# Narrower level products and transposes in a four-layer graph network on one core

## The reference, cut to what matters

```python
x = _layernorm(x + L0(x, edge_index, ...))               # GCN after a two-layer MLP
x = _layernorm(x + L1(x, edge_index, edge_weight, ...))  # two weighted GCN convolutions
x = _layernorm(x + L2(x, src, dst, ...))                 # attention over the edges of a node
x = _layernorm(x + L3(x, src, dst, edge_attr, ...))      # edge MLP, segment sum, update MLP
# inside L0
h = relu(nodes @ W1 + b1) @ W2                           # 64 -> 128 -> 64
msgs = h[src] * norm[:, None]
out = segment_sum(msgs, dst, n) + b2
```

## Time and profile before

| | |
|---|---|
| median of 3 runs | 3193.22 us (3192.8 to 3195.03) |
| span of the profiled execution | 3193.3 us (the profile gives no other time for it) |
| PE busy | 2310.1 us, 72% |
| DVE busy | 2033.0 us, 64% |
| ACT busy | 1390.8 us, 44% |
| POOL busy | 2135.9 us, 67% |
| mean granted clock of PE | 0.864 |

### The profile page before, as it was taken

The page is one execution under the profiler, slowest core; times in us unless marked ns, Lnnn a source line. Parts: engine busy times, 40 slices in busy tenths (PEclk is TensorE's granted clock), DMA queues, the critical chain, the costliest instruction groups (busy, mean ns, idle before and its releaser), DMA issues.

```text
span 3193.3 us, 41332 instructions
## 1 busy us (share of the span) xinstructions
PE 2310.1 (72%) x11332; PEld 1296.4 (41%) x11332; DVE 2033.0 (64%) x4224; ACT 1390.8 (44%) x2605; POOL 2135.9 (67%) x1658
## 2 busy tenths in 40 slices
PE   0678999987767986566567885999666476666665
PEld 0233444433325875454434443444344333333332
DVE  4357888877757865555549995777779733333332
ACT  2576777755433332222224544777533233223232
POOL 6457787788810185888868885888432378888887
PEclk9899999988888998788879997999877577777777
DMA  7894222356544543344434453444256622222221
GB/s 227 252 294 112 54 54 55 70 119 135 120 91 100 120 89 74 81 95 101 97 70 116 114 118 72 104 103 102 70 141 158 154 64 59 54 54 54 54 59 25
DMA packets 598244, 325.99 MB, mean 102 GB/s; under 512 B 510673, under 2 KB 559303, under 8 KB 598020
## 3 DMA queue, kind: packets, MB, share of 16 engines
q1 hardware_dynamic: 524419, 276.68, 33.7%
q0 software_dynamic: 73600, 46.68, 8.8%
HBM read 187.96 MB, written 134.18 MB: 101 GB/s over the span
## 4 chain that ended last, share of the span: by engine, by line
POOL 44%; PE 18%; issue 16%; DMA 8%; DVE 8%; SPq 4%; ACT 2%; DVEq 0%; ACTq 0%; POOLq 0%
POOL g_row L717 34%; POOL out_rows L724 6%; PE bank L831 4%; PE bank L909 4%; DMA x_with_info<-wide 4%; POOL l_a L717 4%; PE pair L889 3%; DVE rT L1526 2%; SPq L600 1%; DMA l_b<-t_x 1%; PE bank L900 1%; PE bank L933 1%; DMA g_row<-t_x,gidx 1%; DVE ss L1452 1%; DVE x_r L1513 1%
## 5 line engine op out<-in xcount | busy, mean ns | idle before, releaser
L717 POOL DMA_INDIRECT g_row<-t_x,gidx x600 | 795.4, 1326 | 237.6 <-issue 201.8
L1142 ACT ACTIVATE hid<-pair,b_up 128x1000 f32<-128x1000 f32 x350 | 378.7, 1082 | 53.6 <-PE pair L890 51.1
L909 PE MATMUL bank<-hid,w_dn 128*64 128x500 f32 x700 | 389.3, 639 | 2.0 <-ACT hid L1142 2.0
L910 PE MATMUL bank<-hid,w_dn 128*64 128x500 f32 x700 | 389.3, 639 | 0.0
L889 PE MATMUL pair<-xT,w_top 64*128 64x500 f32 x500 | 304.1, 691 | 13.9 <-ACT hid L1142 7.3
L717 POOL DMA_INDIRECT g_row<-t_h,gidx x200 | 257.1, 1285 | 79.6 <-issue 60.7
L890 PE MATMUL pair<-xT,w_bot 64*128 64x500 f32 x500 | 304.4, 692 | 0.0
L717 POOL DMA_INDIRECT g_row<-x_with_info,src_i x200 | 259.7, 1299 | 62.3 <-issue 56.7
L724 POOL DMA_INDIRECT out_rows<-n_r,fidx x200 | 248.5, 1242 | 64.8 <-issue 60.3
L724 POOL DMA_INDIRECT x_with_info<-info_r,sidx x200 | 243.1, 1215 | 60.9 <-issue 60.9
L717 POOL DMA_INDIRECT l_a<-in_x,dst_i x88 | 116.5, 1324 | 243.2 <-PE bank L831 216.7
(11 more groups left out here) (264 smaller groups left out, 5618.5 us busy)
## 6 DMA issues: line engine op xcount, KB each, us to landing
x_in<-in_x_cols SPq DMA_DIRECT2D x100, 250.0 KB
x_with_info<-wide SPq DMA_DIRECT2D x50, 476.0 KB
wide<-in_x SPq DMA_DIRECT2D x50, 448.0 KB
out_rows<-x_r SPq DMA_DIRECT2D x100, 224.0 KB
l_k<-keep_row SPq DMA_DIRECT2D x150, 125.0 KB
t_x<-x_r SPq DMA_DIRECT2D x75, 224.0 KB
t_x<-n_r SPq DMA_DIRECT2D x150, 112.0 KB
l_a<-t_x SPq DMA_DIRECT2D x150, 112.0 KB
```

What stands on the lines that cost most here:

```text
L717: return g.indirect_dma_start(out=to, out_offset=None, in_=table, in_offset=bass.IndirectOffsetOnAxis(ap=index[:, tile:tile + 1], axis=0), ...
L909: T.matmul(run.down[0:D, 0:CH], w_dn[a.stage][:, 0:D], hid[a.b2][:, 0, :], start=True, stop=True)
L910: T.matmul(run.down[D:128, 0:CH], w_dn[a.stage][:, 0:D], hid[a.b2][:, 1, :], start=True, stop=True)\
L1142: A.activation(hid[a.b2][:, :, :], run.up[a.b2][:, :, 0:CH], ACT.Relu, bias=b_up[:, a.stage:a.stage + 1]).then_inc(Cn["hid"], 1)
```

## The change

In levels A, B, C and G and in one product of M, matrices and tiles are cut to the columns and rows in use: 64, or 65 where a row of ones carries a bias or a sum. Nothing else is changed; the buffers, their zeros, the waits and the order stay.

```diff
-            def tiles_to_cols(dst, src):
+            def tiles_to_cols(dst, src, width=128):
                 for k in range(TC):
-                    mm = turn(dst[:, k * R:(k + 1) * R], src[:, k * 128:(k + 1) * 128], R, 128)
+                    mm = turn(dst[0:width, k * R:(k + 1) * R], src[:, k * 128:k * 128 + width], R, width)
...
             def cols_to_tiles(dst, src):
                 for k in range(TC):
-                    mm = turn(dst[0:R, k * 128:(k + 1) * 128], src[:, k * R:(k + 1) * R], 128, R)
+                    mm = turn(dst[0:R, k * 128:k * 128 + D], src[0:D, k * R:(k + 1) * R], D, R)
...
-            def down_rows(dst, h, w):
+            def down_rows(dst, h, w, depth=128, width=D):
                 for k in range(TC):
-                    mm = T.matmul(dst[0:R, 128 * k:128 * k + 128], h[:, k * R:(k + 1) * R], w[:, :], start=True, stop=True)
+                    mm = T.matmul(dst[0:R, 128 * k:128 * k + width], h[0:depth, k * R:(k + 1) * R], w[0:depth, 0:width],
+                                  start=True, stop=True)
...
-                    tiles_to_cols(XT, l_a[q]).then_inc(LA["xdT"].sem, 1)
+                    tiles_to_cols(XT, l_a[q], D).then_inc(LA["xdT"].sem, 1)
...
-                    T.matmul(HT[:, 0:CH], w_top[0][:, :], lxT[q][:, :], start=True, stop=True).then_inc(LA["up"].sem, 1)
+                    T.matmul(HT[:, 0:CH], w_top[0][0:D, :], lxT[q][0:D, :], start=True, stop=True).then_inc(LA["up"].sem, 1)
...
-                        mm = T.matmul(AT[0:R, i * 128:(i + 1) * 128], agg[p][:, i * R:(i + 1) * R], cmat[:, :],
+                        mm = T.matmul(AT[0:R, i * 128:i * 128 + D], agg[p][0:D, i * R:(i + 1) * R], cmat[0:D, 0:D],
                                       start=True, stop=True)
...
-                    down_rows(XC, lxT[q], x_up).then_inc(LA["xc"].sem, 1)
+                    down_rows(XC, lxT[q], x_up, D + 1).then_inc(LA["xc"].sem, 1)
...
-                    down_rows(AT, agg[p], g_out).then_inc(LE["aggT"].sem, 1)
+                    down_rows(AT, agg[p], g_out, D + 1, D + 1).then_inc(LE["aggT"].sem, 1)
...
-                        to, tile = OT[0:R, 128 * i:128 * i + 128], slice(i * R, (i + 1) * R)
-                        T.matmul(to, lhid2[p][:, tile], w_dn[2][:, :], start=True, stop=False)
-                        mm = T.matmul(to, l_in[q][:, tile], x_dn[:, :], start=False, stop=True)
+                        to, tile = OT[0:R, 128 * i:128 * i + D], slice(i * R, (i + 1) * R)
+                        T.matmul(to, lhid2[p][:, tile], w_dn[2][:, 0:D], start=True, stop=False)
+                        mm = T.matmul(to, l_in[q][:, tile], x_dn[:, 0:D], start=False, stop=True)
```

More of the change, by code:

```diff
@@ L953, in slot_a @@
                     at_least(pe, LA["agg"], k)
-                    tiles_to_cols(MT, m_r[p]).then_inc(LA["msgT"].sem, 1)
+                    tiles_to_cols(MT, m_r[p], D).then_inc(LA["msgT"].sem, 1)
                     at_least(pe, LA["xcol"], k + 1)
                     at_least(pe, LA["hid"], k)
-                    T.matmul(HT[:, 0:CH], w_top[0][:, :], lxT[q][:, :], start=True, stop=True).then_inc(LA["up"].sem, 1)
+                    T.matmul(HT[:, 0:CH], w_top[0][0:D, :], lxT[q][0:D, :], start=True, stop=True).then_inc(LA["up"].sem, 1)
                 if c := at(2):
@@ L982, in slot_b @@
                     at_least(pe, LB["ucol"], k)
-                    tiles_to_cols(UT, u_r[p]).then_inc(LB["uT"].sem, 1)
+                    tiles_to_cols(UT, u_r[p], D).then_inc(LB["uT"].sem, 1)
                 if c := at(1):
@@ L987, in slot_b @@
                     at_least(pe, LB["agg"], k)
-                    tiles_to_cols(MT, m_r[p]).then_inc(LB["msgT"].sem, 1)
+                    tiles_to_cols(MT, m_r[p], D).then_inc(LB["msgT"].sem, 1)
                 if c := at(2):
@@ L1002, in slot_b @@
                     at_least(pe, LB["hid"], k)
-                    T.matmul(HT[:, 0:CH], w_top[1][:, :], lxT[p][:, :], start=True, stop=True).then_inc(LB["up"].sem, 1)
+                    T.matmul(HT[:, 0:CH], w_top[1][0:D, :], lxT[p][0:D, :], start=True, stop=True).then_inc(LB["up"].sem, 1)
             lagged_slots(slot_b, 5)
@@ L1011, in slot_c @@
                     at_least(pe, LC["agg"], k)
-                    tiles_to_cols(MT, m_r[p]).then_inc(LC["msgT"].sem, 1)
+                    tiles_to_cols(MT, m_r[p], D).then_inc(LC["msgT"].sem, 1)
             def after_c(at):
```

## The result

The change made the kernel slower: 3386.93 us median (3381.19 to 3392.59, 4 runs) against 3194.12 us before on the same chip, a ratio of 1.0594 with a 95% interval of 1.0569 to 1.0620. The profiled execution spans 3390.8 us, 197.5 more than before; its mean granted clock is 0.763 instead of 0.864. Lines of `kernel.py` behind L933 are one higher than before (the up product L957 is now L958, L964 is L965).

What follows compares the result with a forecast made beforehand. PE was taken to bound only A's first half, gathers B, C and M, with DVE busy most of G. The sum was 3193.3 + 184 (A) + 12 (B) + 12 (C, G, M) = 3401 us, range 3206 to 3460.

Steps and rivals of the forecast that it cites:

- The clock in A: Level A: granted clock stays at 0.50, chunks of 8.9 us on PE, +184 us (+150 to +210).
- the likeliest case: Level A: low clock throughout, 3401 us for the whole kernel; chance 0.66.
- The rival with a risen clock: Level A: clock rises as before, 3217 us (3200 to 3245); chance 0.20.
- Its reason: Start of A: no group fills the array any more, so nothing that came before the clock's rise is left.
- The narrow passes: A's 24 passes a chunk streaming 64 columns: paced by weight loads, gaining only 0.10 us a chunk.
- The rival of passes at half their time: A's narrow passes: loads don't bind, 0.055 us a pass, 3177 us; chance 0.05.
- The changes of shape: Level A: three a chunk at 0.145 us, 0.44 at the high clock (0.25 to 0.60); 0.5 at the low.
- the 0.04 us that do go from the fifth group: A's chunk: the fifth group's excess over the fourth, a wait that a later PE hides, 0.04 us less.
- the rival of two passes: A's turned tiles: turning into 64 columns costs two passes, 10.6 us a chunk, 3490 us; chance 0.04.
- B: Level B: at the low clock PE slightly exceeds the gathers, 6.7 us a chunk against 6.5; +12 us (0 to +25).
- C, G and M: These levels: less PE work may lower their clock, mostly covered by other engines; +12 us together (0 to +60).

Runs made afterwards that it cites:

- the kernels with 64 and 65 rows: Kernel before with only A's up product cut from 128 rows of weights to 64 (ratio 1.0025) or to 65 (ratio 1.0005).
- the last burst: Changed kernel plus unread full products in A, back to back: twelve at chunks 4 and 20 (3350.39 us), or eight at each of seven chunks (3297.57 us).

## Why the prediction came out as it did

**The clock in A**, the likeliest case, is what happened: 0.50 throughout, 8.75 us a chunk against 8.9, PE-bound over all 50 chunks, +177 us against +184. The rival with a risen clock gave 3217 us, 24 more than before; the kernel with its up product whole shows what it would have looked like, 20 more (3222.29 us against 3202.26 of before on its chip).

**Its reason was partly wrong.** I wrote that the tiles use half of the columns, the up product half of the rows, and the narrow passes stream half of the time, and that nothing of what preceded the rise is left. The tiles' columns had no part in it: cut alone they change nothing, and made whole in the changed kernel they bring nothing back. Rows and streams together bring the clock down; A's up product alone is enough to bring it up again. Since columns were cut in turned tiles only, it stays open whether columns don't matter or turned tiles matter less than other products. That the clock "never does in A" is true of this kernel, but closer than I thought: once other products had raised it, the same work held it for 56 us.

The Trainium skill ("TensorE: Matmul & The Clock Gate", "What's actually happening") has the clock follow how busy the array has been. Read as the busy time of the profile, the traces disagree: 94.30 of 94.30 us busy, at 0.50 after the change and at 1.00 before.

**The narrow passes** take what they took before, as the earlier trace rows said: 0.21 us at the low clock, 0.109 at the high one. That the load of 125 columns sets this, and not a fixed cost of a pass, is argued: no narrow pass here loads fewer. The gain was put at 0.10 us a chunk and is about 0.05 (4.30 us against 4.35 or 4.36). The rival of passes at half their time (3177 us) is out.

**The changes of shape** were three at 0.145 us, 0.44 a chunk; they are two at 0.17, 0.35. From the last group (65 rows, 128 columns of the array) to the tiles with 64 columns there is none: L933 to L831 takes 1.68 us after the change, eight passes at 0.21. At the low clock they come to 8.75 - 8.38 = 0.37 us, where 8.38 is 2 x 0.835, 1.67 and 3 x 1.68; I took 0.5. With the measured terms, and the 0.04 us that do go from the fifth group, a chunk at the high clock comes to 4.36 - 0.05 - 0.04 + 0.35 = 4.62 us; it is 4.60, forecast 4.66. In the dense chain a group of turned tiles ahead of products of 64 weight columns did take 0.20 more; there two such products run side by side (L909 and L910 start 0.01 us apart), in A nothing runs beside the tiles. Whether that makes the difference isn't shown.

The Trainium skill ("TensorEngine Tiling (Array Packing)", "Key Properties") says that a change of tiling mode drains the engine; the kernels with 64 and 65 rows agree that a change of rows costs time, 0.17 us each, and the change of columns at A's turned tiles shows no cost. That column tiling excludes the transpose mode for float32 ("Gotcha 2: Feature Incompatibilities"), on which the rival of two passes rested, shows no cost here: the tiles into 64 columns take 0.83 us for four at the low clock and 0.43 at the high one, as before.

**B** was put at +12 us, and is +10.7: its clock is 0.50 and PE 312.81 of 320 us busy. **C, G and M** were put at +12 together and are 2.0 + 5.6 + 2.4 = +10.0 with D, whose 1.6 were put at nothing; M's clock, 0.77, didn't fall at all, and G's fell from 0.75 to 0.64 under a DVE that is busy 191.78 of 215 us.

## What to carry to other kernels

Ahead of cutting zeros out of products, look at whether a narrower pass is faster at all: here, with 125 columns of weights loaded for each, a narrower stream paid next to nothing, and 64 rows between products of 128 cost time on each side (0.17 us). Then look at the clock of that stretch: where PE is the bound and busy, the padding may be what keeps the clock high, and one product left at full size (here A's up product) may be enough. Where a product has few rows, 65 instead of 64 kept the shape and cost nothing in the kernel before; in the changed kernel that wasn't tried.

## What the runs showed that was not expected

- More work made the kernel faster: 100 full products that nobody reads took 3386.93 to 3296.64 us (by ratio, 5.94% over before to 3.04%).
- The same narrow work ran at either level of the clock: chunks of 8.75 us at 0.50 and 4.60 us at 1.00; from a risen clock it fell back 8, 8, 22, 27 and 56 us behind the last burst.
- 64 columns of weights in turned tiles changed neither time (ratio 0.9994) nor clock.
